# A gated delta-rule layer with MoE-LoRA: recurrence in chunks of 32 steps instead of 16, part of its products on GpSimd

## The reference

```python
q = silu(causal_dwconv(x @ Wq.T)); k = silu(causal_dwconv(x @ Wk.T)) * DK**-0.5; v = silu(causal_dwconv(x @ Wv.T))
a = sigmoid(x @ Wa.T + ba); beta = sigmoid(x @ Wb.T + bb)
def step(S, xs):                       # 512 times, for each pair
    Sk = einsum('bhvk,bhk->bhv', S, k_t)
    S = a_t[..., None] * S - (b_t[..., None] * (Sk - v_t))[..., None] * k_t[:, :, None, :]
    o_t = einsum('bhvk,bhk->bhv', S, q_t)
o = layernorm(o) * ln_g + ln_b; out = x + (o * sigmoid(x @ Wg.T)) @ Wo.T + ffn(xn)
```

## Time and profile before

| what | us |
|---|---|
| median of 3 runs | 3678.63 |
| the profiled execution's own time | 3682.32 |
| its span, first to last instruction | 3680.6 |
| feed-forward, 0 to 276 | 276 |
| projection, 276 to 985 | 709 |
| setting up the recurrence, 985 to 1023 | 38 |
| recurrence, 1023 to 3258 | 2235 |
| output, 3258 to 3680 | 422 |

### The profile page before, as it was taken

How to read it: one execution, slowest core, us unless ns; L and a number is a source line. 1 busy time by engine, 2 the same in 40 slices (tenths; PEclk the granted TensorE clock), 3 DMA queues, 4 the chain that set the end, 5 groups by cost and what they waited for, 6 DMA issues and landing times.

```text
span 3680.6 us, 59545 instructions
## 1 busy us (share of the span) xinstructions
PE 3323.7 (90%) x18600; PEld 2333.9 (63%) x18600; DVE 2664.3 (72%) x5949; ACT 2319.9 (63%) x6090; POOL 8.9 (0%) x13
## 2 busy tenths in 40 slices
PE   5999888888689989999999999999999998999999
PEld 3557666767556766766766766776776776753333
DVE  4228999999977777777877777777777777832333
ACT  1008788878756666766766767666766766653333
POOL 0000000000000000000000000000000000000000
PEclk9999999999899999999999999999999999999999
DMA  3001222222420010011011011001001001021110
GB/s 148 12 11 69 114 114 114 114 114 118 160 111 36 35 70 36 35 65 42 35 65 41 35 51 55 35 37 70 36 36 70 35 36 70 35 81 52 51 41 33
DMA packets 60020, 231.86 MB, mean 63 GB/s; under 512 B 5264, under 2 KB 16264, under 8 KB 50104
## 3 DMA queue, kind: packets, MB, share of 16 engines
q1 hardware_dynamic: 59656, 227.86, 15.8%
q0 software_dynamic: 48, 0.17, 0.0%
HBM read 123.16 MB, written 104.86 MB: 62 GB/s over the span
## 4 chain that ended last, share of the span: by engine, by line
PE 72%; DVE 14%; issue 10%; ACT 4%; DMA 0%; DVEq 0%; ACTq 0%; SPq 0%
PE PS L1028 14%; PE PS L1010 13%; PE PS L1040 7%; DVE arena L713 7%; PE PS L981 6%; PE PS L986 6%; PE PS L1078 4%; PE PS L1131 3%; PE PS L1119 3%; PE PS L1146 3%; PE PS L942 2%; PE PS L1106 2%; PE PS L1141 2%; PE PS L1053 1%; PE PS L955 1%
## 5 line engine op out<-in xcount | busy, mean ns | idle before, releaser
L543 ACT ACTIVATE arena<-arena 128x128 f32<-128x128 f32 x2048 | 654.2, 393 | 52.9 <-DVE arena L808 52.9
L1028 PE MATMUL PS<-arena 128*128 128x128 f32 x4096 | 559.2, 279 | 49.1 <-ACT arena L533 49.1
L972 PE MATMUL PS<-XNT,arena 128*128 x2048 | 499.2, 404 | 104.0 <-ACT arena L469 101.4
L1010 PE MATMUL PS<-arena 128*128 128x256 f32 x2048 | 563.1, 399 | 26.8 <-issue 26.8
L1028 PEld LDWEIGHTS PS<-arena 128*128 128x128 f32 x4096 | 506.7, 191 | 125.8 <-ACT arena L524 62.4
L972 PEld LDWEIGHTS PS<-XNT,arena 128*128 128x128 f32 x2048 | 402.9, 198 | 192.1 <-ACT arena L469 117.0
L713 DVE SCALAR_TENSOR_TENSOR arena<-arena,SM 128x256 f32<-128x256 f32 x1152 | 464.6, 493 | 15.3 <-ACT arena L469 15.3
L1010 PEld LDWEIGHTS PS<-arena 128*128 128x128 f32 x2048 | 374.6, 199 | 135.6 <-issue 93.1
L808 DVE TENSOR_TENSOR arena<-arena,PS 128x512 f32<-128x512 f32 x512 | 349.8, 683 | 142.3 <-PE PS L1010 139.0
L524 ACT COPY arena<-PS 128x64 f32<-128x64 f32 x1024 | 199.7, 278 | 287.8 <-PE PS L1028 252.9
L533 ACT COPY arena<-PS 128x512 f32<-128x512 f32 x512 | 300.3, 586 | 116.0 <-PE PS L1040 96.3
(11 more groups left out here) (140 smaller groups left out, 4235.4 us busy)
## 6 DMA issues: line engine op xcount, KB each, us to landing
arena<-kq_d SPq DMA_DIRECT2D x33, 1024.0 KB, 4.8
kq_d<-arena SPq DMA_DIRECT2D x8, 4096.0 KB, 11.5
...
```

The source lines that it names most:

```text
L543: ins = nc.scalar.mul(S[:, p, :], S[:, p, :], ACH[c][:, p:p + 1])
L972: ins = mm(bank(g % 8)[:, cols * k:cols * (k + 1)], w, XNT[:, kt, bass.ds(c * PC + (HALO + PC - cols), cols)], start=(kt == 0), stop=(kt = ...
L1010: ins = mm(bank(7)[:, 256 * a:256 * (a + 1)], PTZ[:, r, s, :], KTB[d][:, s].rearrange("r e k -> r (e k)"), start=True, stop=True)
L1028: ins = mm(bank(5)[:, 4 * NI * q:4 * NI * (q + 1)].rearrange("v (i p) -> v i p", p=4), STR[:, j % 2, a, e, :], KQ[d][:, :, p0:p0 + 4], sta ...
```

## The change

- **Chunks.** The recurrence goes in 16 chunks of C = 32 steps, 8 blocks of 4 steps each; the loop has 7 turns of two chunks, and the last two chunks are written out. The last chunk neither updates nor reads the states.
- **Corrections by levels.** After block m a correction goes only as far as LEVEL[m] steps: 4, 8, 4, 16, 4, 8, 4, and 32 (the state) at the end. Its products are made on tiles of 32 rows, four beside each other in the array (functions level_products, chunk_products, corrections, carried), with the weights in PTL and PT32. Updates of the state are also on 32 rows (update), so PTZ goes.
- **GpSimd.** It makes the elementwise key products (products, before L764), the outputs (outputs: 3 instructions a block), and the decays of later blocks of X (decay: of 1, 2, 4, 1, 1, 2 and 1 blocks, 512 elements each). In the projection it multiplies keys by beta (8 instructions of 512 elements a chunk) and makes suffix products of a (4 of 1024, 2 of 256, 2 of 128, 2 of 64).
- **Broadcast by DRAM.** The sums of key products leave PSUM through a tile GS, go to DRAM (g_d) and come back over all partitions as GB, 512 KB for a block. Values, decays and suffix products (VAS) are loaded block by block, and the outputs stored block by block from the same slots.
- **VectorE in a block** (functions add, dec, weigh, sub, in this order): add 0, dec 0, weigh 0, add 1, sub 0, weigh 1, dec 1, add 2, sub 1, weigh 2, dec 2, add 3, P, sub 2, copy. Between them stand the subtractions of corrections from PSUM (16 head_sub of 256 elements a chunk, 12 level_sub of 512), 16 state_add of 512, 3 key_mask of 512, and 7 extensions of P (256, 256, 512, 256, 256, 512, 1024).
- **Projection.** XNT is held by sequence; silu is one ScalarE function, written straight to staging in runs of 4 steps; the jobs of a (16 sigmoids) stand at the end of a chunk, those of beta are gone (beta is made once, before the feed-forward block, and comes back from DRAM). VectorE is left with the taps.
- **Output.** The same instructions; OC is held by blocks of 4 steps, so that a head's columns lie in runs of 4.

The core of the diff (nested functions of build):

```diff
-C = 16
-BL = 4
-NB = C // BL
-NSUP = T // C
...
+C = 32
+BL = 4
+NB = C // BL
+NS = T // C
+BP = BL * NP
...
+LEVEL = [4, 8, 4, 16, 4, 8, 4, 32]
...
+NEST_BEFORE = [1, 2, 4, 4, 5, 6, 7]
...
+U_AT = [[], [0, 1], [2], [3, 4], [5], [6], [7], []]
...
+READ_AT = [[], [0], [1, 2, 3], [4, 5], [6, 7, 8], [9, 10, 11], [12, 13], [14, 15]]
+PREP_AT = [[], [], [("ones", 2, 4), ("g2", 0, 5)], [("kt", 0, 4), ("g2", 1, 5)], [("kt", 1, 4), ("ones", 3, 5)],
+           [("gl", 16, 4)], [("kt", 2, 4), ("gl", 8, 4), ("ones", 0, 5)], [("kt", 3, 4), ("gl", 4, 4), ("ones", 1, 5)]]
...
+            def load_gb(n, m):
+                sp.wait_ge(g_stored, n * 64 + (16 * (m // 2) + 16))
+                sp.dma_start(GB[:, m % 4].rearrange("v p x -> v (p x)"), g_d[at(n), 16 * NP * m:16 * NP * (m + 1)].to_broadcast([128, 16 * NP])).then_inc(gb_in[m % 4], 16)
+            def store_gs(n, w, item):
+                sp.wait_ge(pa_done, item)
+                sp.dma_start(g_d[at(n), 2048 * w:2048 * (w + 1)].rearrange("s (c x) -> (s c) x", c=4), GS[0:128:32, :]).then_inc(g_stored, 16)
...
+                    pool.wait_ge(silu_done, c * NQ + 3 + x + 1)
+                    pp = slice(16 * (x - NQ // 3), 16 * (x - NQ // 3) + 16)
+                    for s in range(PSC):
+                        kb = KBS[:, s, pp]
+                        tt(kb, KQST[:, pp, NB * s:NB * (s + 1), 0, :], kb, ALU.mult).then_inc(kb_step, 1)
+                pool.wait_ge(job_free, c * NJ + 8 + NJ)
+                pool.wait_ge(sf_stored, c * 16 + 16)
+                tt(S4[:, :, 1], A4[:, :, 2], A4[:, :, 3], ALU.mult).then_inc(sf_step, 1)
+                nc.gpsimd.tensor_copy(S4[:, :, 2], A4[:, :, 3]).then_inc(sf_step, 1)
+                pool.wait_ge(sf_step, c * 10 + 2)
...
+            def products(q, c, count):
+                pr = PR[:, q % 2]
+                later = [pr[:, :, 0:6].rearrange("k p (e t) -> k p e t", e=2), pr[:, :, 6:10].rearrange("k p (e t) -> k p e t", e=2),
+                         pr[:, :, 10:12].rearrange("k p (e t) -> k p e t", e=2)]
+                for s in range(3):
+                    key = KB[c][:, :, 4 * q + s].unsqueeze(2).unsqueeze(3).to_broadcast([128, NP, 2, 3 - s])
+                    tt(later[s], KQ[c][:, q, :, :, s + 1:4], key, ALU.mult).then_inc(pr_step, 1)
+                tt(pr[:, :, 12:16], KQ[c][:, q, :, 1, :], KB[c][:, :, 4 * q:4 * q + 4], ALU.mult).then_inc(pr_step, 1)
+                pool.wait_ge(pr_step, count * 4 + 4)
+                nc.gpsimd.nop().then_inc(pr_ready, 1)
...
+                def decay(lo, hi, factor):
+                    xs = Xc[:, lo:hi].rearrange("v l p e t -> v l p (e t)")
+                    tt(xs, xs, factor.unsqueeze(1).unsqueeze(3).to_broadcast([128, hi - lo, NP, 2 * BL]), ALU.mult).then_inc(nested, 1)
...
+                def outputs(m):
+                    k = n * 24 + 3 * m
+                    pool.wait_ge(x_sub, n * NB * 3 + (3 * m + 3))
+                    tt(OT, Xc[:, m, :, 0, :], GB[:, m % 4, :, 12:16], ALU.mult).then_inc(o_step, 1)
+                    ov = VAS[:, m % 4, 0]
+                    tt(ov, VAS[:, m % 4, 1], Xc[:, m, :, 1, :], ALU.mult).then_inc(o_step, 1)
+                    pool.wait_ge(o_step, k + 2)
+                    tt(ov, OT, ov, ALU.subtract).then_inc(o_step, 1)
...
+                    if m == 0:
+                        pool.wait_ge(e_in[c], i * 16 + 16)
+                        pool.wait_ge(vas_in[0], n * 32 + 16)
+                        pool.wait_ge(corr_sub, n * N_SUB + 4)
+                        decay(1, 2, block_decay(0))
+                        next_products(0)
+                        pool.wait_ge(corr_sub, n * N_SUB + 12)
+                        decay(2, 4, EX[c][:, 0])
+                    elif m == 1:
+                        pool.wait_ge(corr_sub, n * N_SUB + 16)
+                        decay(4, 8, EX[c][:, 4])
+                    elif m == 2:
...
+                    if m > 0:
+                        outputs(m - 1)
+                        if m == 4:
+                            pool.wait_ge(corr_sub, n * N_SUB + SUB_AT[3] + 4)
+                            decay(6, 8, EX[c][:, 2])
+                        next_products(m)
...
+                    dst = VST[:, pp] if x >= 2 * NQ // 3 else KQST[:, pp, :, 1 - x // 4, :]
+                    nc.scalar.activation(dst, ACC[:, x % 3].rearrange("p h b (l t) -> p (h b) l t", t=BL), ACT.Silu).then_inc(silu_done, 1)
...
+                def head_sub(b, hf):
+                    dst = Xc[:, b, 32 * hf:32 * hf + 32].rearrange("v (g j) e t -> v g j (e t)", j=4)
+                    src = PS[:, 2048 * hf:2048 * (hf + 1)].rearrange("v (j g l x) -> v l g j x", j=4, g=8, l=NB)[:, b]
+                    dve.wait_ge(corr_full, n * 9 + 1 + hf)
+                    tt(dst, dst, src, ALU.subtract).then_inc(corr_sub, 1)
...
+                def level_sub(m, k):
+                    L = LEVEL[m]
+                    dst = Xc[:, m + 1 + k].rearrange("v (g j p) e t -> v g j (p e t)", j=4, p=32 // L)
+                    src = PS[:, 0:2048].rearrange("v (j x) -> v j x", j=4)[:, :, 0:32 * L].rearrange("v j (g l x) -> v l g j x", g=L // 2, l=L // 4)[:, k]
+                    dve.wait_ge(corr_full, n * 9 + 2 + m + 1)
+                    dve.wait_ge(nested, n * 7 + NEST_BEFORE[m])
+                    tt(dst, dst, src, ALU.subtract).then_inc(corr_sub, 1)
...
+                def state_add(s):
+                    j, g0 = slot_pairs(s)
+                    dst = S.rearrange("v (g j) k -> v j g k", j=4)[:, j, g0:g0 + 4]
+                    dve.wait_ge(up_psum, n * 8 + s // 2 + 1)
+                    tt(dst, dst, bank(4 + s % 2).rearrange("v (g k) -> v g k", g=4), ALU.subtract).then_inc(s_updated, 1)
...
+                        tt(W[:, :, t], V[:, :, t], W[:, :, t], ALU.add).then_inc(v_add, 1)
...
+                        xs = Xb[:, :, :, t + 1:4]
+                        tt(xs, xs, A[:, :, t].unsqueeze(2).unsqueeze(3).to_broadcast([128, NP, 2, 3 - t]), ALU.mult).then_inc(x_dec, 1)
...
+                        a, w = (0, 6, 10)[t], 6 - 2 * t
+                        tt(TMP[:, :, 0:w], GB[:, sl, :, a:a + w], W[:, :, t].unsqueeze(2).to_broadcast([128, NP, w]), ALU.mult).then_inc(wg_mul, 1)
...
+                        xs = Xb[:, :, :, t + 1:4]
+                        tt(xs, xs, TMP[:, :, 0:6 - 2 * t].rearrange("v p (e t) -> v p e t", e=2), ALU.subtract).then_inc(x_sub, 1)
...
+                    tt(Pt[:, :, at:at + 3], W[:, :, 0:3], SF[:, :, 0:3], ALU.mult).then_inc(p_head, 1)
+                    sub(2)
+                    dve.wait_ge(x_sub, k3 + 3)
+                    nc.vector.tensor_copy(Pt[:, :, at + 3], W[:, :, 3]).then_inc(p_ready, 1)
...
+            def block_products(w, bk, pr_count):
+                pe.wait_ge(pr_ready, pr_count)
+                for r in range(4):
+                    ins = mm(bank(bk)[32 * r:32 * r + 32, :], ones[:, 0:32], PR[:, r // 2, 32 * (r % 2):32 * (r % 2) + 32, :].rearrange("k p x -> k (p x)"), start=True, stop=True)
+                ins.then_inc(pa_full, 1)
...
+                    for gi in range(4):
+                        for b in range(2):
+                            j, g0 = slot_pairs(2 * u + b)
+                            rows = slice(32 * j, 32 * j + 32)
+                            ins = mm(bank(4 + b)[:, 128 * gi:128 * (gi + 1)], PT32[rows, g0 + gi, :], KBT[rows, g0 + gi, :], start=True, stop=True)
+                    ins.then_inc(up_psum, 1)
...
+                    for g in range(G):
+                        for j in range(4):
+                            rows = slice(32 * j, 32 * j + 32)
+                            ins = mm(bank(j)[:, 64 * g:64 * (g + 1)], PTL[rows, 128 * g:128 * (g + 1)], GL[L][rows, 64 * (s * G + g):64 * (s * G + g + 1)], start=True, stop=True)
+                    ins.then_inc(corr_full, 1)
```

1227 lines of the change are left out of this document (683 added, 544 removed).

## The result

| | before | after |
|---|---|---|
| median, us | 3680.1 (6 runs, 3677.8 to 3683.3) | 3466.4 (6 runs, 3458.6 to 3496.1) |
| ratio, 95% interval | | 0.9429 [0.941, 0.9447] |
| profiled execution, us | 3682.3 | 3496.1 |
| mean granted TensorE clock | 0.954 | 0.733 |

The change saves 5.7%, some 214 us. The forecast was 3221. One of run 13's four executions, of 3393.5 us, was in a slow state and is left out of its time.

A forecast was written before the change was run, and what follows sets the result against it. It took TensorE to bound recurrence and output, VectorE the projection. Feed-forward with beta 278, projection 772, setting up 48, recurrence 1753 and output 368 sum to 3219, plus 1.7 outside the span: 3221 us, range 2700 to 3700.

The forecast's parts named there:

- chunk of 111: Recurrence: a 32-step chunk takes 111 us, from 104.6 for VectorE and GpSimd, 5 for packing, 1.3 for the loop.
- the formula 2218 + 400 p: Whole kernel: forecast time in us as a function of p, GpSimd's price in ns an element.
- Covered in a chunk: Recurrence: TensorE (45 to 81 us), ScalarE (51 to 54) and handoff waits (up to 29) fit below 111 us.
- 45.4 and 59.2 us: Recurrence, a chunk: VectorE's instructions with two SBUF inputs and GpSimd's work, added as mutually exclusive to 104.6 us.
- VectorE's own 71 us: Recurrence: VectorE's instructions in a chunk take 71 us unhindered, against 108 now for two supersteps.
- GpSimd's price of 2.5 ns: GpSimd's two-input work: 2.5 ns an element, three times its memset's price, making 59 us a chunk in the recurrence.
- Exclusion: Recurrence and projection: VectorE's two-SBUF-input instructions and GpSimd's shut each other out; 45.4 plus 59.2 us a recurrence chunk; chance 0.5.
- Projection 772: Projection: 8 chunks of 96.5 us (58 taps, 16.4 standstill, 22 exclusion) make 772 us instead of 709.
- Setting up 48: Setting up: suffix products, store, memsets, products, TensorE with copy, and the DRAM round trip make 48 us instead of 38.
- Output 368: Output stage: 128 passes of L1131 get 0.42 us cheaper each, 54 us in all, giving 368 us instead of 422.
- Rival 1: VectorE and GpSimd don't hinder each other: recurrence chunk 89.4 us, projection 595, total time 2704 us; chance 0.27.
- Rival 3: Recurrence: TensorE's quarter tiles don't work side by side, chunk 145 us, total about 3600; or uncovered handoffs, total 2890; chance 0.1.

The follow-up runs named there:

- run 13: The change with state decays moved to VectorE and each block's last state read behind its corrections, without the spare multiplies of run 12: 3337 us, 0.905 of before.
- run 2: The change with all two-input GpSimd operations in projection and recurrence replaced by constant fills, those computations left out: 3008 us, 0.816 of before.
- run 12: The change with state decays on VectorE, 20 unread TensorE multiplies in block 1, last state read behind the corrections: 3215 us, 0.874 of before.

## Why the prediction was wrong

The direction was right and the size was not: 5.7% against 12.5%. Against the 274 us that are missing in all, the recurrence alone has 364, 24 us in each chunk of 111; the projection gives 138 back. That 3466 lies inside the stated range of 2700 to 3700 is luck: the range was made wide for GpSimd's price, the formula 2218 + 400 p would need 3.1 ns for it, and GpSimd was busy for 60.7 us a chunk where 59.2 had been forecast.

**The step that failed** is "Covered in a chunk". It has TensorE at "45 to 81 us" under 111, and the wait for transposes, copy and correction "comes 8 times a chunk, between nothing and 29 us, and lies under GpSimd's work". TensorE took 93 us, and GpSimd's work does not cover the waits: VectorE idles 40 us a chunk, above the 29, and 42 when GpSimd has little to do (run 2). I had added 45.4 and 59.2 us as if one of the two engines always worked. But the chain VectorE, TensorE, ScalarE, TensorE, VectorE stops the next block, and GpSimd's outputs soon after, so a wait lies beside the hindrance and not under it. What was measured in a chunk is VectorE's own 69, hindrance 26 and waits 40: 135.

**The term that was missing** is the clock. TensorE's prices came from rows at 0.96, and the changed kernel runs its recurrence at 0.61. At the low level a group of 32 correction records takes 1.99 us for 1.12 and four transposes 1.04 for 0.66 (run 12 above). TensorE's 93 us are outside 45 to 81 for that reason: a line through its busy time in the two chunk rows of the change (81.7 at 0.70, 97.4 at 0.57), over the inverse of the clock, gives 63 at 0.96, an estimate. What the low clock costs in all I can only estimate, by a line of chunk length over the inverse of the clock through the rows above. For the change it is 36.2 us for each unit (127.2 at 0.70, 139.0 at 0.57) and gives 113 us at 0.96, 22 less than 135. For run 2 it is 48.7 (102.7 at 0.80, 120.4 at 0.62) and gives 93 instead of 111.5, 19 less. Over 16 chunks that is 300 to 350 of the 364 us. It reaches beyond the clocks seen, so it is no measurement; what is measured is run 13 against run 12, 122 us for 0.13 of clock. If the estimate holds, the forecast's 111 would have been about right at the old clock, but by luck, as two errors cancel: 14 us too much hindrance (40 for 26) and some 20 of waits left out.

**Point by point.**
- VectorE's own 71 us: 69.3 in run 2. Right.
- GpSimd's price of 2.5 ns: 59.2 us forecast, 60.7 with its waits for VectorE inside. For 2048 elements it is cheaper, 1.9 ns an element (L525 above). The Trainium skill (GPSIMD Engine Reference, Performance versus the Vector engine) has 2.2 ns for an fp32 add; the trace is a little below.
- Exclusion: right in kind. dec 0 has 0.87 us, forecast near 1, and PSUM readers keep 0.68. The rule of the Trainium skill (SBUF — State Buffer, Who interferes with whom), by which the dear end holds, agrees in kind. But it costs 26 us a chunk and not 40. Part of GpSimd's work may fall into VectorE's waits; how much was not measured.
- Projection 772: it is 634. Exclusion was spread over all taps, 22 us a chunk. Back-to-back taps keep their 0.397 us and it is GpSimd that waits, L470 5.26 us on average for what takes it 1.27 in most instances; VectorE loses 11 us, once, where it comes out of a wait into GpSimd's suffix products. ScalarE's 16 sigmoids take 5.95 us instead of 9.9.
- Setting up 48: it is 73. GpSimd's suffix products begin only at 916, and the TensorE work that follows the memsets ran at 0.57.
- Output 368: 396. L1131's passes did get cheaper: 68.5 us for 128 (L1403) against 120.0, 51 us, forecast 54. But the gate's weights are loaded only after the recurrence, and TensorE waits 18.2 us for that load. The last 7 us of the 28 stay open.
- Rival 1 (no hindrance, 2704) is what run 2 built: 3008, its chunk 111.5 instead of 89.4. It failed by the same step.
- Rival 3 (TensorE, about 3600) named the right engine and the wrong reason: at the low clock 62 correction passes on 32 rows take 3.66 us (L1313 above), 0.06 each, where it had up to 0.13 and the forecast 0.02 to 0.03. Quarter tiles do run side by side, and the forecast's price fits at the high clock (32 in 1.12 us, run 12).
